# Sparse and dense attention of a fused transformer kernel: the low parts' product joins the scores, in rows 48 to 61 of each half of the array

## The reference, cut to what matters

```
# sparse attention, per head: 512 strided keys (every 8th token) and the own block of 128
w = softmax(concat(q @ k_str.T, q_block @ k_block.T) / 4 + mask)
o = w @ concat(v_str, v_block)
# dense attentions, per head, over all 4096 tokens, causal
attn = softmax(where(causal, Q @ K.T / 4, -inf));  y = attn @ V
# layer 1, the second: q and k are normalised per head first
```

## Time and profile before

| | us |
|---|---|
| median of 3 runs | 5110.38 |
| lowest and highest run | 5086.99, 5111.56 |
| span of the profiled execution | 5116.3 |
| TensorE busy in it | 4781.3 (93%) |
| VectorE busy | 4006.1 (78%) |
| ScalarE busy | 2867.2 (56%) |
| GpSimd busy | 241.8 (5%) |

### The profile page before, as it was taken

How to read it: one execution, slowest core, us unless ns; L and a number is a source line. 1 busy time by engine, 2 the same in 40 slices (tenths; PEclk the granted TensorE clock), 3 DMA queues, 4 the chain that set the end, 5 groups by cost and what they waited for, 6 DMA issues and landing times.

```text
span 5116.3 us, 82733 instructions
## 1 busy us (share of the span) xinstructions
PE 4781.3 (93%) x31872; PEld 2539.4 (50%) x31872; DVE 4006.1 (78%) x9075; ACT 2867.2 (56%) x3349; POOL 241.8 (5%) x259
## 2 busy tenths in 40 slices
PE   6699997868999999999999999999999999899999
PEld 5455555754434344433334433334443333688888
DVE  8677775767898988888888989988899875555555
ACT  4356554433566766666666667666567677332232
POOL 5200001110000000000000000000000000300000
PEclk9799898877899999999999999999899999899999
DMA  6622223765000201200300300300300000210010
GB/s 192 175 77 69 65 51 105 230 221 97 16 11 14 48 16 32 43 9 5 50 13 21 58 9 5 50 13 20 54 11 8 9 7 7 71 42 21 21 42 9
DMA packets 259185, 258.36 MB, mean 50 GB/s; under 512 B 78288, under 2 KB 198096, under 8 KB 257440
## 3 DMA queue, kind: packets, MB, share of 16 engines
q1 hardware_dynamic: 250784, 212.86, 14.8%
q0 software_dynamic: 6240, 38.80, 4.7%
q10 hardware_dynamic: 1768, 1.42, 0.2%
HBM read 145.44 MB, written 105.97 MB: 49 GB/s over the span
## 4 chain that ended last, share of the span: by engine, by line
PE 73%; DVE 19%; issue 5%; ACT 2%; SPq 1%; DMA 1%; DVEq 0%; ACTq 0%
PE psum L885 24%; PE psum L813 20%; PE psum L76 14%; DVE maxes_dense L951 11%; PE psum L845 4%; PE psum L777 3%; PE psum L802 2%; PE psum L823 1%; PE psum L854 1%; PE psum L1656 1%; DVE masked_scores_dense L944 1%; PE psum L809 1%; PE psum L1636 0%; PE psum L864 0%; ACT probs_dense L908 0%
## 5 line engine op out<-in xcount | busy, mean ns | idle before, releaser
L908 ACT ACTIVATE probs_dense<-psum 128x1024 f32<-128x1024 f32 (+3 forms) x2304 | 2068.1, 950 | 1042.2 <-PE psum L845 755.1
L951 DVE TENSOR_REDUCE maxes_dense<-psum 128x1 f32<-128x512 f32 x3584 | 2227.5, 684 | 232.1 <-PE psum L813 231.3
L813 PE MATMUL psum<-keys,queries_dense 48*128 48x512 f32 (+3 forms) x4608 | 1553.0, 477 | 114.6 <-DVE maxes_dense L951 22.1
L813 PEld LDWEIGHTS psum<-keys,queries_dense 48*128 48x128 f32 x4608 | 668.2, 191 | 1471.4 <-DVE maxes_dense L951 1143.6
L885 PE MATMUL psum<-probs_dense,values 128*32 128x512 f32 (+3 forms) x9216 | 1181.2, 591 | 0.0
L845 PE MATMUL psum<-queries_dense,keys 50*128 50x512 f32 (+3 forms) x4608 | 809.7, 407 | 11.5 <-ACT probs_dense L908 11.2
L944 DVE CUSTOM_DVE_ANT_0 masked_scores_dense<-psum,causal_add 128x128 f32<-128x128 f32 (+3 forms) x1024 | 452.4, 488 | 151.5 <-PE psum L813 132.2
L845 PEld LDWEIGHTS psum<-queries_dense,keys 50*128 50x128 f32 x4608 | 449.6, 193 | 106.4 <-ACT probs_dense L908 60.0
L944 DVE CUSTOM_DVE_ANT_0 masked_scores_sparse<-psum,after_add 128x512 f32<-128x512 f32 x512 | 326.2, 687 | 99.9 <-PE psum L802 99.0
L1763 ACT ACTIVATE activated<-psum 128x512 f32<-128x512 f32 x208 | 124.4, 598 | 417.5 <-PE psum L76 405.8
L885 PEld LDWEIGHTS psum<-probs_dense,values 128*32 128x32 f32 x9216 | 189.9, 109 | 273.1 <-issue 203.0
(11 more groups left out here) (296 smaller groups left out, 5252.6 us busy)
## 6 DMA issues: line engine op xcount, KB each, us to landing
v_scratch<-ve_s SPq DMA_DIRECT2D x96, 256.0 KB, 3.5
queries_dense<-parts_scratch SPq DMA_DIRECT2D x384, 64.0 KB
keys<-parts_scratch POOLq DMA_DIRECT2D x42, 512.0 KB, 18.0
parts_scratch<-part_high SPq DMA_DIRECT2D x16, 1024.0 KB, 4.3
parts_scratch<-part_low SPq DMA_DIRECT2D x16, 1024.0 KB, 7.1
values<-v_scratch POOLq DMA_DIRECT2D x8, 2048.0 KB, 35.3
queries_sparse<-parts_scratch SPq DMA_DIRECT2D x192, 64.0 KB
own_keys<-parts_scratch SPq DMA_DIRECT2D x192, 64.0 KB
```

The costliest lines, as they stand in the source:

```text
L813: m = pe.matmul(bank[:, 0:width], q[rows(h, TROWS), h // 2, b * P:(b + 1) * P], k[rows(h, TROWS), h // 2, kc * STRIP:kc * STRIP + width], ...
L908: act.activation(probs[i % 6][:, :, first_col:STRIP], psum[:, at2:at2 + 2, first_col:STRIP], ACT.Exp, scale=SCALE, **extra).then_inc(exp_d ...
L951: m = dve.tensor_reduce(mx[:, h * BLOCKS + b, kc:kc + 1], bank, AX.X, ALU.max)
```

## The change

A fourth term joins the list: low x low, with as many dimensions as there is room for. A half of the array has 64 rows; two are kept for the maxima, so the products have 62 (`TROWS`), of which 48 hold the three terms and 14 the first 14 of the 16 dimensions of the low parts' product. The rows of the maxima and of the ones move from 48 and 49 to 62 and 63. The first pass uses 62 rows, the second 64. Each load of queries, keys and strided keys has one DMA more for each half of the rows, with 14 rows. The counts of the semaphores follow.

```diff
-TERMS = ((0, 0), (0, 1), (1, 0))
-TROWS = len(TERMS) * HEAD_DIM
+HALF = P // 2
 MROWS = 2
-SROWS = TROWS + MROWS
-HALF = P // 2
+TROWS = HALF - MROWS
+SROWS = HALF
+TERMS = ((0, 0, HEAD_DIM), (0, 1, HEAD_DIM), (1, 0, HEAD_DIM), (1, 1, TROWS - 3 * HEAD_DIM))
...
-        per_unit = 16 * 15 if sparse else 16 * 8
-        earlier = 0 if sparse else 4 * 16 * 15
+        per_unit = 16 * 19 if sparse else 16 * 10
+        earlier = 0 if sparse else 4 * 16 * 19
...
-                return per_unit * (n // 8) + 16 * 13
-            return earlier + per_unit * (n // 8) + 16 * 12
+                return per_unit * (n // 8) + 16 * 17
+            return earlier + per_unit * (n // 8) + 16 * 16
...
             def load_keys(queue, group, tokens, loaded):
                 a, g = groups[group]
                 for odd in range(2):
-                    for i, (_, part) in enumerate(TERMS):
+                    for i, (_, part, dims) in enumerate(TERMS):
                         src = parts_d[a][part][DIM + g * GROUP * HEAD_DIM:DIM + (g + 1) * GROUP * HEAD_DIM, tokens]
                         first_row = odd * HALF + i * HEAD_DIM
-                        queue.dma_start(keys[group % 2][first_row:first_row + HEAD_DIM, :, tokens].bitcast(F32),
-                                        src.rearrange("(h o e) t -> o e h t", o=2, e=HEAD_DIM)[odd]).then_inc(loaded, 16)
+                        queue.dma_start(keys[group % 2][first_row:first_row + dims, :, tokens].bitcast(F32),
+                                        src.rearrange("(h o e) t -> o e h t", o=2, e=HEAD_DIM)[odd, 0:dims]).then_inc(loaded, 16)
...
-                    pe.wait_ge(keys_in[group % 2], 96 * ((group + 1) // 2))
+                    pe.wait_ge(keys_in[group % 2], 128 * ((group + 1) // 2))
...
-                                pe.wait_ge(str_in[n // STRIPS], 16 * 7)
+                                pe.wait_ge(str_in[n // STRIPS], 16 * 9)
```

More of the change, by code:

```diff
@@ L692, in load_strided @@
                 for odd in range(2):
-                    for i, (_, part) in enumerate(TERMS):
+                    for i, (_, part, dims) in enumerate(TERMS):
                         src = str_d[part][g * GROUP * HEAD_DIM:(g + 1) * GROUP * HEAD_DIM, :]
                         first_row = odd * HALF + i * HEAD_DIM
-                        queue.dma_start(str_keys[g][first_row:first_row + HEAD_DIM, :, :].bitcast(F32),
-                                     src.rearrange("(h o e) t -> o e h t", o=2, e=HEAD_DIM)[odd]).then_inc(str_in[g], 16)
+                        queue.dma_start(str_keys[g][first_row:first_row + dims, :, :].bitcast(F32),
+                                     src.rearrange("(h o e) t -> o e h t", o=2, e=HEAD_DIM)[odd, 0:dims]).then_inc(str_in[g], 16)
                 queue.dma_start(str_values[g][:], v_d[0][g].rearrange("(c p e) n -> p c e n", p=P, e=STRIDE)
@@ L706, in load_queries @@
                     for odd in range(2):
-                        for i, (part, _) in enumerate(TERMS):
+                        for i, (part, _, dims) in enumerate(TERMS):
                             src = parts_d[a][part][g * GROUP * HEAD_DIM:(g + 1) * GROUP * HEAD_DIM, j * STRIP:(j + 1) * STRIP]
                             first_row = odd * HALF + i * HEAD_DIM
-                            sp.dma_start(queries[n % held][first_row:first_row + HEAD_DIM, :, :].bitcast(F32),
-                                         src.rearrange("(h o e) t -> o e h t", o=2, e=HEAD_DIM)[odd]).then_inc(queries_in[n % 8], 16)
+                            sp.dma_start(queries[n % held][first_row:first_row + dims, :, :].bitcast(F32),
+                                         src.rearrange("(h o e) t -> o e h t", o=2, e=HEAD_DIM)[odd, 0:dims]).then_inc(queries_in[n % 8], 16)
                     if not sparse and n < STRIPS:
@@ L715, in load_queries @@
                         for odd in range(2):
-                            for i, (_, part) in enumerate(TERMS):
+                            for i, (_, part, dims) in enumerate(TERMS):
                                 src = parts_d[a][part][DIM + g * GROUP * HEAD_DIM:DIM + (g + 1) * GROUP * HEAD_DIM, j * STRIP:(j + 1) * STRIP]
                                 first_row = odd * HALF + i * HEAD_DIM
-                                sp.dma_start(keys[n % held][first_row:first_row + HEAD_DIM, :, :].bitcast(F32),
-                                             src.rearrange("(h o e) t -> o e h t", o=2, e=HEAD_DIM)[odd]).then_inc(queries_in[n % 8], 16)
+                                sp.dma_start(keys[n % held][first_row:first_row + dims, :, :].bitcast(F32),
+                                             src.rearrange("(h o e) t -> o e h t", o=2, e=HEAD_DIM)[odd, 0:dims]).then_inc(queries_in[n % 8], 16)
                         sp.dma_start(values[n % held][:], v_d[a][g, j * STRIP:(j + 1) * STRIP, :].rearrange("(b p) n -> p b n", p=P)).then_inc(queries_in[n % 8], 16)
```

## The result

The changed kernel takes 5075.42 us (median of 9 runs, 5068.43 to 5084.92), the kernel before 5104.06 us beside it (9 runs, 5084.52 to 5115.25). In the profiled executions the spans are 5116.3 and 5066.3 us, 50.0 us apart: the profiled execution of the kernel before lies above all nine of its runs here, that of the changed kernel is the fastest of its nine, so spans put the gain too high and the medians' 28.6 us are the measure. Ratios are taken between runs made beside each other and over fast runs alone, which left out two of the four runs on 34 rows, so a ratio is not always the quotient of the medians printed.

The account below looks back on a forecast made before the run. TensorE, busy for 93% of the span, was taken as the bound; added loads cost 11.7 + 3 + 5.5 = 20.2 us on the 5110.4 us median, giving 5130.5 us (+0.40%), with a range of 5106 to 5156 us.

Parts of the forecast that it names:

- The first term: Products of both attention passes: going from 48 to 62 and 50 to 64 rows costs 0 us.
- The prediction's own sign of being wrong: One of the listed signs: a granted clock that moved by more than 0.01 over dense attention.
- The rival that held: Clock rises with fuller array: 16 us regained in sparse, 80 us in dense attention, 5034 us; chance 0.08.
- Head of sparse attention: SP's queue before the first hand-over of the maxima: 22 more DMAs at 0.534 us, 11.7 us.
- Units of sparse attention: SP's added loads per unit, mostly hidden by slack before hand-overs: 3 us, bounds 0.4 and 6.4.
- Head of dense attention: Transfers queued ahead of the first dense hand-over grow: 5.5 us, bounds 4.4 and 7.4.
- The rest of dense attention: SP's added loads hidden by waits for VectorE, POOL's group loads by starting some 400 us ahead: 0 us.
- The prediction's price for this cover gone: Dense attention's group loads on POOL, if not hidden: 0.9 MB at 170 GB/s, 5 us once a group.
- Slow issues: Rival on SP in sparse attention and the dense head: a 14-row DMA costs 0.61 us; +44 us, 5155 us; chance 0.17.

Follow-up runs that it names:

- the loads alone: The changed kernel with the 14 new rows loaded but read by no product, matmuls staying at 48 and 50 rows: 5149.86 us, ratio 1.0066.
- with zeros: The kernel before on 62 and 64 rows, the 14 added rows holding zeros written once into every tile: 5061.15 us, ratio 0.9894.

## Why the prediction was wrong

**Where the time came from.** The clock's worth can be had in three ways. By closure on the spans: 50.0 us of span and 37.4 us of added waits, 87.4 us; from the loads alone to the change, 86.7 us of span with waits within 0.2 us of each other. By closure on many runs, which is the fairer: 28.6 us between the medians and 37.4 us of waits, 66 us; from the loads alone to the change the ratios differ by 0.0116, 59 us. And by the kernel before itself, whose 57 runs beside these experiments lie between 5076.4 us at a mean clock of 0.944 and 5145.5 us at 0.926: a line through them has 4.1 us for each 0.001 (correlation -0.97). The loads alone have a median clock of 0.932 over their runs, the change 0.952: 0.020 x 4100 = 82 us, where the medians differ by 74.4 us. So the rows were worth 60 to 90 us, and that two closures on single executions agree within 1 us is luck: one program's runs are up to 69 us apart.

**The first term failed.** "No row shows more time for more rows, so 48 to 62 and 50 to 64 rows are put at nothing." The rows cited the earlier trace rows do not contradict that, and neither do those after. But a group's mean duration is taken at whatever clock was granted, and tells nothing of what sets the clock. With both passes on more rows the term measured -60 to -90 us, and it alone turned the sign of the forecast. The Trainium skill, TensorE: Matmul & The Clock Gate, section "Why this matters for your kernels", says that a single matmul on 32 rows takes the time of one on 128. Near one clock this case agrees: 496 ns on 48 rows at 0.95, 487 ns on 62 rows at 0.98. It does not carry over to a stage whose clock moves with the rows: on 34 and 36 rows the means are 695 and 592 ns at 0.59, on 62 and 64 rows 487 and 416 ns at 0.98. There the measurement decides. The prediction's own sign of being wrong, a granted clock that moves by more than 0.01 over dense attention, came: 0.95 to 0.98.

**The rival that held** was given 0.08: "If what holds it is how full the array is, 62 rows in place of 48 lift it." Its price was 16 us in sparse attention and 80 us in dense attention, 96 in all. By the spans of the stages, with the added waits of each, sparse attention and the middle stage gave 24.1 + 9.0 = 33 us and dense attention 23.4 + 28.4 = 52 us: the total was near, its parts were not. Its 5034 us lie 41 us below the measured 5075: the clock gave about 66 us by the medians and not 96, the loads took 37 and not 20, and the kernel before stood at 5104 and not 5110. What I held against it, 0.95 beside 0.97 "nearly the same", was a comparison of stages with different work. The evidence for it was in front of me: three units of 24 us and 0.72 beside others of 18.8 us, on an engine as busy as ever. I had no row that varied the rows alone, and should have read that as a wide bound, not as nothing.

**Head of sparse attention**, 11.7 us forecast: 4.3 + 4.7 = 9.0 us. The hand-over came at 225.91 - 178.95 = 47.0 us behind the first load instead of 39.0, 8.0 us later and not 11.7, because 95 DMAs took 0.494 us each and not 0.534: the slow issues didn't grow with the count. No run shows whether a full queue was what made some of them slow. TensorE's two waits grew by 9.0 us in all, 1.0 us more than the hand-over's delay, so the first tile's 4.3 us lies inside it nearly whole, as forecast.

**Units of sparse attention**, 3 us forecast: about nothing. The slack before a hand-over fell to 0.04 us at 281.36, and its waits on SP from 129.0 to 61.5 us, but behind the first hand-over TensorE waited for only three more, 0.8 us in all. The distance of 1 us that the forecast gave the landing was hardly needed.

**Head of dense attention**, 5.5 us forecast: 1.7 + 5.6 = 7.3 us, at the upper bound. The forecast had the hand-over's wait at about 17 us, and it was 17.1; the first tile's 1.7 us it had left out.

**The rest of dense attention**, 0 us forecast, "hidden": 13.8 + 7.3 = 21.1 us. This is the second failed step. It was priced by when group loads are needed, 400 us ahead, and not by whom they keep waiting while they move: SP's loads for the second hand-over, and the stores of `aos_dense`, for which VectorE and then TensorE wait. The prediction's price for this cover gone, 5 us once a group, is near the 4.6 us of each of the three waits by luck: it was the price of keys that come late, and no keys did. Why SP's second hand-over was late is shown in part only: its loads took 10.5 us to issue beside GpSimd's, and the wait went when those were cut smaller.

**Slow issues**, 0.17: the 14-row load costs 0.42 us, as taken. The Trainium skill, DMA: Bandwidth & Descriptors, section "Why a DMA increments its semaphore by 16 and not by 1", has the issuing queue write the missing increments itself; if it does so for 14 rows, no time of it shows here. The loads together cost 34 us instead of 20, by the ratio of the loads alone, which by themselves are the slower kernel.

## What to carry to other kernels

Look at the granted clock by stage before counting instructions. Where TensorE is the bound, busy almost without a gap, and still below 1.00, as in sparse attention here, try a change that fills more rows of the array: here it paid even with zeros (0.9894), and saving rows cost a quarter (1.2492). Price a load not only by when its data are needed but by what moves beside it: put what the bounding engine needs next ahead in the queue, and cut large loads and spread them over time.

## What the runs showed of the hardware that was not expected

- The granted clock of this kernel, on one core, depends on the rows in use: 0.669 on 34 and 36, 0.907 on 42 and 44, 0.934 on 48 and 50, 0.945 on 54 and 56, 0.951 on 62 and 64. Zeros do as well as ones or data.
- Which property of the matmuls it goes by (the rows of the weights, those of the moving operand, one pass or the mean over all) was not separated further. The products on 64 rows for masks and on 128 rows for the values are in all of these kernels, and their share was not varied.
- In 57 runs of the unchanged kernel before the mean clock of a run moves between 0.926 and 0.944, and with it the time by 69 us. Most of the spread of this kernel's runs is the clock's.
- A load on 14 rows takes SP 0.42 us to issue like one on 16. Beside GpSimd's loads of group 1, eight loads of keys took 10.5 us instead of the 3.5 to 3.7 us that most such eights take.
